# Layer norm in a four-layer network: the four blocks of squares are added by TensorE's matmuls instead of by VectorE

## The reference

```
def _layernorm(x, axis=-1, eps=1e-05):
    m = jnp.mean(x, axis=axis, keepdims=True)
    v = jnp.var(x, axis=axis, keepdims=True)
    return (x - m) / jnp.sqrt(v + eps)
...
xn = _layernorm(x, axis=-1)
x = x + _L1_attn_ref(xn, ...) + _L1_ffn_ref(xn, ...)
```

## Time and profile before

| what | value |
|---|---|
| time, median of 3 runs | 2467.77 us (2457.39 to 2469.15) |
| time of the profiled execution | 2459.2 us |
| its span, first to last instruction | 2457.4 us |
| TensorE matmul busy | 2354.0 us, 96% |
| VectorE busy | 1614.1 us, 66% |
| ScalarE busy | 1158.5 us, 47% |
| mean granted clock of TensorE | 0.983 |

### The profile page before, as it was taken

How to read it: one execution, slowest core, us unless ns; L and a number is a source line. 1 busy time by engine, 2 the same in 40 slices (tenths; PEclk the granted TensorE clock), 3 DMA queues, 4 the chain that set the end, 5 groups by cost and what they waited for, 6 DMA issues and landing times. The chain is left out here.

```text
span 2457.4 us, 37984 instructions
## 1 busy us (share of the span) xinstructions
PE 2354.0 (96%) x12732; PEld 1881.9 (77%) x12732; DVE 1614.1 (66%) x2607; ACT 1158.5 (47%) x2219; POOL 648.0 (26%) x460
## 2 busy tenths in 40 slices
PE   5999999899989999999999899999999999999898
PEld 4777777688866668888777788888888877888665
DVE  5796467854477775655555587777777776543585
ACT  3333146533247443135555476666666654322573
POOL 2132020245221334736666300000000023430010
PEclk8999999999989999999999999999999999999999
DMA  2132175222343222234444432232222222332421
GB/s 90 47 120 87 40 134 103 35 42 43 54 96 67 46 38 44 33 120 159 158 162 162 146 100 64 77 94 85 88 65 77 77 39 38 53 48 39 102 63 44
DMA packets 406200, 195.19 MB, mean 79 GB/s; under 512 B 280392, under 2 KB 359728, under 8 KB 406078
## 3 DMA queue, kind: packets, MB, share of 16 engines
q1 hardware_dynamic: 404860, 191.53, 31.2%
q10 hardware_dynamic: 1218, 2.06, 0.4%
HBM read 129.85 MB, written 44.04 MB: 71 GB/s over the span
## 5 line engine op out<-in xcount | busy, mean ns | idle before, releaser
L643 PE MATMUL banks<-xn_hi,w_hi 128*128 128x512 f32 x784 | 309.7, 395 | 8.5 <-ACT sgf L1183 5.5
L643 PE MATMUL banks<-xn_hi,w_lo 128*128 128x512 f32 x784 | 306.3, 391 | 0.0
L643 PE MATMUL banks<-xn_lo,w_hi 128*128 128x512 f32 x784 | 306.1, 390 | 0.0
L631 DVE TENSOR_TENSOR w_lo<-tw,w_hi 128x512 fp32r<-128x512 f32 (+2 forms) x136 | 125.0, 925 | 201.6 <-ACT w_hi L623 201.5
L503 POOL TENSOR_TENSOR nat<-nat,wscale 128x512 f32<-128x512 f32 (+1 forms) x44 | 50.8, 1162 | 654.2 <-DMA nat<-in_L_ffn_w 654.2
L1304 POOL TENSOR_TENSOR h_lo<-sgf,h_hi 128x512 fp32r<-128x512 f32 (+1 forms) x94 | 128.1, 1367 | 337.7 <-ACT h_hi L1186 337.7
L643 PEld LDWEIGHTS banks<-xn_hi,w_hi 128*128 128x128 f32 x784 | 147.7, 188 | 41.0 <-DVE w_lo L631 5.8
L3098 POOL TENSOR_TENSOR ssq<-ssq,sq 128x1024 f32<-128x1024 f32 x59 | 145.6, 2467 | 103.7 <-ACT sq L2913 98.6
L643 PEld LDWEIGHTS banks<-xn_hi,w_lo 128*128 128x128 f32 x784 | 147.5, 188 | 31.1
L643 PEld LDWEIGHTS banks<-xn_lo,w_hi 128*128 128x128 f32 x784 | 147.8, 188 | 29.4
L623 ACT ACTIVATE w_hi<-tw 128x512 fp32r<-128x512 f32 (+2 forms) x136 | 78.9, 587 | 190.6 <-PE banks L643 105.7
(11 more groups left out here) (337 smaller groups left out, 6454.1 us busy)
## 6 DMA issues: line engine op xcount, KB each, us to landing
qk_scratch<-raw SPq DMA_DIRECT2D x64, 512.0 KB, 2.7
qk_raw<-qk_scratch SPq DMA_DIRECT2D x64, 512.0 KB, 3.8
nat<-in_L_ffn_w SPq DMA_DIRECT2D x48, 256.0 KB
head_scratch<-stage SPq DMA_DIRECT2D x16, 512.0 KB, 3.3
st_qs<-st_hi SPq DMA_DIRECT2D x128, 64.0 KB, 2.0
nat<-in_L_attn_Wq SPq DMA_DIRECT2D x32, 256.0 KB
nat<-in_L_attn_Wk SPq DMA_DIRECT2D x32, 256.0 KB
nat<-in_L_attn_Wv SPq DMA_DIRECT2D x32, 256.0 KB
```

Source lines behind the costliest of these rows:

```text
L631: ins = nc.vector.tensor_tensor(w_lo[r, j, c], src[r, c], w_hi[r, j, c].bitcast(F32), ALU.subtract)
L643: mm = nc.tensor.matmul(to[half][:, :], w[0:n, j, k * P:(k + 1) * P], r, start=first and k == 0 and x == 0, stop=last and k == len(rows) - ...
```

## The change

`dve_squares` and its four calls (L983, L1246, L1995, L2003) are left out. `pe_var` waits for the four centred blocks and then, block by block, for ScalarE's squares, and does four one-column matmuls for each of the four blocks: sixteen in place of four, all adding up in the same four columns of PSUM. The first of them alone carries the start flag. `step_d` counts three steps fewer for each half, and the later waits on it are renumbered.

```diff
-                (step_a, 3 * NH), (step_b, NH * KT), (step_c, NH * (KT + 1)), (step_d, NH * 2 * KT), (step_e, NH * KT)))
+                (step_a, 3 * NH), (step_b, NH * KT), (step_c, NH * (KT + 1)), (step_d, NH * (KT + 1)), (step_e, NH * KT)))
...
-        def dve_squares(dve, s, half):
-            for k in range(1, KT):
-                dve.wait_ge(step_c.sem, s.c0 + (KT + 1) * half + k + 1)
-                if k > 1:
-                    dve.wait_ge(step_d.sem, s.d0 + 2 * KT * half + k - 1)
-                nc.vector.tensor_tensor(s.sq[:, 0, :], s.sq[:, 0, :], s.sq[:, k, :], ALU.add).then_inc(step_d.sem, 1)
-
         def pe_var(pe, s, half):
 
-            pe.wait_ge(step_d.sem, s.d0 + 2 * KT * half + KT - 1)
-            for tt in range(TTS):
-                mm = nc.tensor.matmul(acc[1][half][:, tt:tt + 1], s.sq[:, 0, tt * P:(tt + 1) * P], cst[:, C_MEAN:C_MEAN + 1],
-                                      start=True, stop=True)
+            pe.wait_ge(step_b.sem, s.b0 + KT * (half + 1))
+            for k in range(KT):
+                pe.wait_ge(step_c.sem, s.c0 + (KT + 1) * half + k + 1)
+                for tt in range(TTS):
+                    mm = nc.tensor.matmul(acc[1][half][:, tt:tt + 1], s.sq[:, k, tt * P:(tt + 1) * P], cst[:, C_MEAN:C_MEAN + 1],
+                                          start=k == 0 and tt == 0, stop=k == KT - 1 and tt == TTS - 1, skip_group_check=True)
             mm.then_inc(step_a.sem, 1)
...
-            pe.wait_ge(step_d.sem, s.d0 + 2 * KT * half + KT)
+            pe.wait_ge(step_d.sem, s.d0 + (KT + 1) * half + 1)
...
-                act.wait_ge(step_d.sem, s.d0 + 2 * KT * half + KT + k + 1)
+                act.wait_ge(step_d.sem, s.d0 + (KT + 1) * half + k + 2)
...
             evacuate(1)
-            dve_squares(dve, s, 0)
             dve_lo(dve, up, 0, 0, ALL)
...
             dve_gated(dve, s, 0)
-            dve_squares(dve, s.norm, 1)
             dve_inverse(dve, s.norm, 1)
...
             dve_centre(dve, norm, 0)
-            dve_squares(dve, norm, 0)
             low(0)
...
             dve_centre(dve, norm, 1)
-            dve_squares(dve, norm, 1)
             low(3)
```

## The result

The changed kernel takes 2477.01 us (median of 6 runs, 2471.92 to 2479.07) against 2463.45 us for the kernel before (median of 6, 2457.39 to 2469.15): a ratio of 1.0054, 95% interval 1.0036 to 1.0071. The profiled execution took 2471.92 us with a span of 2470.1 us, 12.7 us more than the span of before.

The account below looks back on a forecast made before the run. TensorE, at 96% of the span, was taken as the bound; + 8.2 us for the places at equal clock and + 4 us for the clock made + 12 on 2459.2: 2471 us profiled, 2479 us median, range 2465 to 2489 us.

Parts of the forecast that it names:

- The price of a pass: Variance matmuls on TensorE: 0.111 us a pass at full clock, so 24 more passes add 2.67 us in each of eight places.
- rival 4: Variance passes wait for each other, adding into the same four columns: + 4.4 us in each place, + 35 us; chance 0.02.
- What is saved: TensorE's wait for VectorE's additions in norms 1 to 3, 1.58 to 2.23 us a place, all goes except a 0.04 gap.
- The clock: Behind the variance places: 5 or 6 of 7 fall to 1.2 GHz, against 3 before, at 1.8 us each: + 4 us net.
- rival 3: One-column passes act like idleness: clock falls in all seven places, + 21 us, or + 13.6 with short falls; chance 0.18.
- Rival 1: The clock holds behind the variance places, as no wait is left ahead of the passes: + 2.4 us, 2470 us; chance 0.13.
- Norm 0 half 0: First variance place: 32 passes end at 35.95 against 35.98 before, so 0, or + 2.1 us at the low clock.
- The shift goes to the end: Everything behind a place hangs on TensorE's end, so the delay of the places, + 8.2 us at equal clock, reaches the end.
- Forecast on the median: Whole kernel: the same + 12 us set on the 2467.8 us median of three runs, giving 2479 us.

Follow-up runs that it names:

- one_block: The changed kernel with the variance made of block 0's squares alone, four one-column matmuls and no additions (output not the layer norm): ratio 0.9926 to the kernel before.
- after_wide: The changed kernel with 128 equal columns in place of one as moving operand of its sixteen variance matmuls: ratio 0.9987 to the kernel before.
- before_wide: The kernel before with 128 equal columns in place of one in its four variance matmuls: ratio 0.9981 to the kernel before.
- norm0_old: The changed kernel with both halves of norm 0 as before (three VectorE additions, four variance matmuls): ratio 1.0025 to the kernel before.
- hybrid: The changed kernel, but in norms 1 to 3 VectorE adds two blocks and TensorE takes block 3 meanwhile; norm 0 as before: ratio 0.9965 to the kernel before.
- hybrid_wide: The hybrid with 128 columns in each variance matmul: ratio 0.9956 to the kernel before.

## Why the prediction was right, and where it was off

The forecast was + 12 us on the profiled execution, and 12.7 us came; the median is 2477.0 us against 2479. The chance for slower by over 0.5% was put at 0.45; the ratio of 1.0054 lies just beyond that line, and its interval holds it. The mechanism (24 more weight loads, less the wait, and more falls of the clock) is borne out. That the number agrees to less than 1 us is in part luck: two errors in the clock's term cancelled, and so did three shifts that the sum did not have (the last but one point).

- **The price of a pass**, 0.111 us from the weight loads: right. 24 more passes cost 2.66 us in one_block against after_wide, 2.67 forecast. Passes that wait for each other (rival 4) are excluded: 32 passes took 3.68 us, where 3.56 + 0.11 was forecast.
- **What is saved**: right. At equal clock (after_wide against before_wide, with 8.95 for norm 3 half 1, where the clock fell) a place got longer by 9.57 - 8.32 = 1.25 us in half 0 (1.24 forecast; in norm 2 9.57 - 8.43 = 1.14, 1.18 forecast), 9.57 - 8.95 = 0.62 in half 1 (0.6), 9.57 - 6.89 = 2.68 in norm 0 half 1 (2.67). Together 67.28 - 59.11 = 8.2 us in the seven places, 8.2 forecast.
- **The clock**: right in its direction, off in both factors, which cancelled by luck. 5.6 falls at 1.8 us were forecast. It was 7, and against the flat column of after_wide they cost 77.63 - 67.28 = 10.35 us, 1.5 us each; the product was put at 10. The falls of before cost 2.66, 1.54 and 1.60 us against 8.95, 8.43 and 8.95, together 5.8 (5.8 forecast); with 0.1 us less in the places without a fall, 64.83 - 59.11 = 5.7. So 8.2 + 10.35 - 5.7 = 12.8 us, the difference of the two columns. In its count this is not the forecast but the second half of rival 3, a short fall at every place, which was priced at + 13.6 us. That one-column passes count for little was read from a single place, norm 2 half 0; after_wide shows it.
- **Rival 1, the clock holds**, with the advice of the Trainium skill behind it ("TensorE: Matmul & The Clock Gate", section "Why this matters for your kernels"): it did not. The change did close every idle gap, and the clock fell more often. Closing the gaps was not enough; what filled them had to move columns too, and with 128 columns in each pass the clock held.
- **Norm 0 half 0**: mis-sized in this pair. It was put at 0 with a bound of + 2.1 us. From the first square to the load of the `w_lo` product it took 45.74 - 30.00 = 15.7 us against 44.27 - 31.58 = 12.7: + 3.0 us. The clock fell at 33.4, in the middle of the passes. The timeline of the changed kernel from 32.2 to 33.2 us, ahead of the fall, and from 34 to 36, behind it:

```profile
32.06 1.31 PEld L902 LDWEIGHTS banks<-cst,ln_sq 128*128 128x128 f32 x11 [0.24 <-issue]
...
33.79 2.47 PEld L902 LDWEIGHTS banks<-cst,ln_sq 128*128 128x128 f32 x11
```

  A pass takes (1.31 - 0.19) / 10 = 0.112 us ahead of the fall and (2.47 - 0.33) / 10 = 0.214 us behind it. The prediction's 0.178 us for the low clock is a mixture, since the first of those 8 loads ran at full clock; with 0.214 its bound would have been 32 x 0.103 = 3.3 us. The + 3.0 is also against a lucky execution. The four other executions whose norm 0 is summed by VectorE (norm0_old, before_wide, hybrid, hybrid_wide) took 14.5 to 14.8 us there: their 8 loads took 1.78 us and not 0.97, and started 4.5 us behind the first square and not 3.5. Against them this place cost about 1 us.
- **"The shift goes to the end"**: true. In the last transposes the changed kernel is 2464.15 - 2449.96 = 14.2 us behind (the starts of the same weight load of L827). That is 12.8 + 3.0 for the places, less 1.6 us by which the squares of norm 0 started earlier (30.00 against 31.58; they start between 29.6 and 31.7 in the nine profiled executions, so this is no effect of the change). Between the places the two executions gain and lose up to 3 us at a time, and that adds up to nothing. The span shows 12.7 and not 14.2 since the last transfers of the output landed faster, 2.1 to 2.2 us behind their issue against 2.5 to 3.6; the last took 3.6 us in the kernel before (L839, issue to landing).
- **Forecast on the median**: I set the sum on a median of 2467.8 us from three runs. More runs of the kernel before have their median at 2463.4 to 2463.8, so the level was 4 us too high and hid that the measured difference of medians is 13.6 us, not 12.

What stays open: after_wide gained 16.5 us on the changed kernel. The seven places account for 10.35 us and norm 0 half 0 for 15.7 - 12.2 = 3.5 us more. The profiled executions themselves are only 9.7 us apart in span, since the one of the changed kernel is its fastest (5.1 us under the median) and that of after_wide is 2.4 us over its own. What the clock does between the places differs from execution to execution, and what sets it there is not shown. Work at half the clock loses half of its time, so the clock can give back at most (99.8 - 56.8) / 2 = 21.5 us, with the reserve on the low time above.

## What to carry to other kernels

Before matmuls of few columns are moved onto TensorE to fill its wait, price them by their weight loads, not by their columns, and subtract the wait place by place: at equal clock a wait of 1.5 us did not pay for 24 weight loads (2.67 us), and a place without a wait paid in full. Then look at the granted clock and not at the busy share behind each place: here matmuls of one column kept TensorE busy and lost the clock, and 128 columns of the same operand cost no time and kept it. In the whole kernel that was worth more (16.5 us) than the choice of the engine: with 128 columns on both sides additions and matmuls came to the same time as far as these runs can tell. A mix (two additions by VectorE, a quarter of the squares taken by TensorE meanwhile) beat both pure forms.

## What the runs showed of the hardware that I had not expected

- 32 passes of fp32 with one column and with 128 columns take the same 3.68 us at full clock.
- With one column the clock fell at 13 of the 13 places from norm 0 half 1 on that had 32 such passes (7 in the changed kernel, 6 in norm0_old); with 128 columns at none of 7. With 8 one-column passes and no wait (one_block) it fell at none of 7 either.
- A weight load of these fp32 passes follows the one before at 0.112 us at full clock and at 0.214 us at the low one.
- 16 fp32r matmuls of 128 columns (one pass each) take 1.90 us, the same as 8 fp32 matmuls (16 passes): the number of weight loads sets the time.
- The kernel before shows 86.7 us of a mean execution at the low clock, and wider variance matmuls alone, which compute nothing new, brought it to 74.1 us and the ratio to 0.9981.
